# Two attention layers and two feed-forwards on one core: the first feed-forward's matmuls in three rounded parts, and copies and sums of the second half in another order

## The reference, cut to what matters

```python
x = x + L0_xattn(layernorm(x), ctx)   # attention over features, 8 heads, a band of +-64; gated by ctx
x = x + L0_ffn(layernorm(x))          # only the 32 best of the 64 positions of each row
x = x + L1_xattn(layernorm(x), ctx)   # 32 heads in 8 groups, keys and values from ctx
x = x + L1_ffn(layernorm(x))          # squared relu, plus a gate-weighted expert, layer norm after it

def L0_ffn(x):
    scores = x @ w_r + b_r
    idx = top_k(scores, 32)           # per row
    h = gelu(x[idx] @ w1 + b1)        # 256 -> 1024
    return zeros.at[idx].set(h @ w2 + b2)   # 1024 -> 256
```

## Time and profile before

| what | us |
|---|---|
| median of 3 runs (334.99 to 337.39) | 335.25 |
| the profiled execution | 335.92 |
| its span in the profile | 334.2 |
| what lies outside the span (335.92 - 334.2) | 1.7 |
| TensorE, busy | 309.2 |
| VectorE, busy | 237.7 |
| ScalarE, busy | 198.6 |
| GpSimd, busy | 181.4 |

### The profile page before, as it was taken

The page is one execution under the profiler, slowest core; times in us unless marked ns, Lnnn a source line. Parts: engine busy times, 40 slices in busy tenths (PEclk is TensorE's granted clock), DMA queues, the critical chain, the costliest instruction groups (busy, mean ns, idle before and its releaser), DMA issues.

```text
span 334.2 us, 7216 instructions
## 1 busy us (share of the span) xinstructions
PE 309.2 (93%) x2178; PEld 241.2 (72%) x2178; DVE 237.7 (71%) x921; ACT 198.6 (59%) x415; POOL 181.4 (54%) x294
## 2 busy tenths in 40 slices
PE   6997989998999999999998998879899999999992
PEld 4976667676777777776687875657666578888892
DVE  6778889999999999984246156755788647662264
ACT  4758988887777787868531324566678944104210
POOL 6648566677776957577514414243443831336643
PEclk9999999999999999999999999999999999999999
DMA  6999020202010101100000000000000000000000
GB/s 194 365 372 341 8 49 2 50 1 49 3 41 8 38 13 28 26 1 3 2 0 0 2 0 0 0 2 1 2 1 2 0 2 0 3 32 15 19 31 31
DMA packets 13302, 14.51 MB, mean 43 GB/s; under 512 B 2513, under 2 KB 11985, under 8 KB 13265
## 3 DMA queue, kind: packets, MB, share of 16 engines
q1 hardware_dynamic: 12688, 13.72, 13.0%
q10 hardware_dynamic: 576, 0.33, 0.3%
HBM read 10.64 MB, written 1.05 MB: 35 GB/s over the span
## 4 chain that ended last, share of the span: by engine, by line
PE 61%; POOL 13%; DVE 11%; issue 8%; ACT 6%; POOLq 0%; DVEq 0%; ACTq 0%
PE S L772 6%; PE S L432 5%; PE O L459 5%; PE ST L443 4%; PE ST L797 4%; PE S L566 4%; PE S L648 2%; PE S L715 2%; POOL rstd L1081 2%; POOL hT L1097 2%; PE PJ L692 2%; DVE masked L1294 2%; PE O L729 2%; PE PJ L395 2%; PE O L597 2%
## 5 line engine op out<-in xcount | busy, mean ns | idle before, releaser
L1294 DVE CUSTOM_DVE_ANT_0 masked<-S,band 128x192 bf16<-128x192 f32 x256 | 79.6, 353 | 8.9 <-PE S L432 6.9
L893 ACT ACTIVATE ex<-ST 128x384 f32<-128x384 f32 x128 | 60.9, 491 | 17.7 <-PE ST L443 16.3
L1078 POOL TENSOR_SCALAR rstd<-mv 128x1 f32<-128x1 f32 x40 | 12.1, 303 | 76.1 <-DVE mv L1231 75.5
L432 PE MATMUL S<-qk 128*128 128x384 f32 x128 | 52.1, 408 | 0.8 <-DVE mw L1294 0.4
L443 PE MATMUL ST<-qk 128*128 128x192 f32 x256 | 48.1, 271 | 2.5 <-ACT ex L893 2.0
L443 PEld LDWEIGHTS ST<-qk 128*128 128x128 f32 x256 | 44.9, 189 | 5.0 <-issue 4.4
L1138 POOL TENSOR_SCALAR_AFFINE_SELECT ex<-ex 128x512 f32<-128x512 f32 x32 | 20.4, 639 | 29.6 <-ACT ex L893 29.5
L459 PE MATMUL O<-ex,v 128*32 128x192 f32 x512 | 34.1, 338 | 0.0
L432 PEld LDWEIGHTS S<-qk 128*128 128x128 f32 x128 | 24.1, 188 | 13.3 <-issue 11.4
L1426 DVE TENSOR_REDUCE mw<-S 128x8 f32<-128x512 f32 x32 | 22.0, 686 | 13.0 <-PE S L648 13.0
L863 ACT ACTIVATE hs<-PJ,sb,byhead 128x512 fp32r<-128x512 f32 x29 | 22.6, 779 | 11.5 <-PE PJ L396 10.6
(11 more groups left out here) (204 smaller groups left out, 720.6 us busy)
## 6 DMA issues: line engine op xcount, KB each, us to landing
qk<-kp SPq DMA_DIRECT2D x48, 48.0 KB
w<-in_w SPq DMA_DIRECT2D x2, 1024.0 KB, 10.0
cx<-in_cx SPq DMA_DIRECT2D x1, 1024.0 KB, 9.7
up<-in_up SPq DMA_DIRECT2D x1, 1024.0 KB, 11.8
down<-in_down SPq DMA_DIRECT2D x1, 1024.0 KB, 10.9
out<-x SPq DMA_DIRECT2D x8, 128.0 KB, 1.7
cxT<-in_cxT SPq DMA_DIRECT2D x1, 768.0 KB, 6.1
x<-in_x SPq DMA_DIRECT2D x1, 768.0 KB, 7.9
```

The costliest lines, as they stand in the source:

```text
L432: mm(out, r32(qp[:, t % 2, g, b, P * c:P * c + P]), r32(mv_), start=True, stop=True).then_inc(s["pe_s"], 1)
L893: A(ex[:, (n // 2) % 4, 2 * w:2 * w + 2, :], ST[n % 2][:, 0:2 * WIN].rearrange("p (h k) -> p h k", h=2), ACT.Exp, scale=SCALE).then_inc(s[ ...
L1294: last = V.tensor_tensor_reduce(out=masked[:, n % 2, h, :], in0=S[n % 2][:, WIN * h:WIN * h + WIN], in1=band[:, c, :], scale=1.0, scalar=N ...
```

## The change

1. The matmuls of `ffn_up` and `ffn_down` run in three rounded parts: high x high, high x low and low x high, where high is the value rounded to fp32r and low the rest. 64 fp32 matmuls become 192 rounded ones of the same 256 columns. The parts have to be made:
   - of the up weights by ScalarE (a copy of 128 x 512 at l = 10 of tiles 2 to 5) and GpSimd (a subtract at l = 13 of the same tiles), into the new `w1s`; of the down weights by ScalarE (four casts, in slots (7,12), (7,14), e = 12 and e = 13) and VectorE (subtracts at e = 2, 3, 13, 14), into a free part of `qk`;
   - of the gathered tokens by ScalarE and VectorE, for tiles 0 to 3 at once in tile 7's slots 2 and 3, for tiles 4 to 7 one by one at each `take` (one copy and one subtract more);
   - of the hidden layer by ScalarE after every gelu (a copy into a ring of four buffers in `qk`) and VectorE (`ffn_low`, a subtract one slot later).
2. The steps stand in other slots: tables `UP0`, `GELU0`, `DOWN0` for the first half; up and gelu of the second half at e = 31 to 38 and its downs at e = 34 to 41 (n = -14 to -7); scatters at e = 29, 31, 43, 44, so that all eight stand ahead of n = 0; `ffn_out` at e = 28 and 42.
3. VectorE, not GpSimd, normalises tiles 6 and 7 for the choice.
4. In the second attention L1032 moves from the end of a slot to its start on ScalarE, and the exponential's table load from n = 2 to n = -6. GpSimd's sum `x` + beta moves from the last stage into the second attention's slots (n = 21 + 4t, into `cx`). The gate's two VectorE instructions of tiles 5 to 7 move ahead of the tile before's final instruction.
5. The second feed-forward's weights are loaded into `w1` and `w2` once their parts have been made, not into buffers of their own at the start.

The core of the diff:

```diff
+        SCATTER = {29: (0, 1), 31: (2, 3), 43: (4, 5), 44: (6, 7)}
+        UP0, GELU0 = (9, 10, 13, 14, 16, 18, 20, 22), (11, 12, 13, 14, 16, 18, 20, 22)
+        DOWN0 = (15, 17, 19, 21, 23, 25, 26, 27)
...
-                for k in range(2):
-                    last = mm(up_bank(f), w1[:, k, P * f:P * f + P], xsT[:, k, T * half:T * half + T], start=(k == 0), stop=(k == 1))
+                for i, (k, a, b) in enumerate(PARTS):
+                    last = mm(up_bank(f), r32(w1s[:, a, k, P * f:P * f + P]), r32(x_part(g, b)[:, k, :]),
+                              start=(i == 0), stop=(i == len(PARTS) - 1))
...
-                last = mm(down_bank(c), hT[:, f, P * c:P * c + P], w2[:, f, :], start=(f == 0), stop=(f == FC - 1))
+                pe.wait_ge(s["f_lo"], FC * g + f + 1)
+                for m in range(2):
+                    for i, (a, b) in enumerate(((0, 0), (1, 0), (0, 1))):
+                        last = mm(down_bank(2 * g + m), r32(ffn_h(f, a)[:, P * m:P * m + P]), r32(w2s[:, f, b, :]),
+                                  start=(f == 0 and i == 0), stop=(f == FC - 1 and i == 2))
...
+                A(hT[:, f, 0:T], up_bank(f), ACT.Gelu_apprx_tanh, bias=b1[:, f:f + 1]).then_inc(s["fa_up"], 1)
+                if m >= 4:
+                    act.wait_ge(*ring_last(m))
+                A(r32(ffn_h(f, 0)), hT[:, f, 0:T], ACT.Copy).then_inc(s["fa_hi"], 1)
...
+            def ffn_low(g, f):
+                dve.wait_ge(s["fa_hi"], FC * g + f + 1)
+                V.tensor_tensor(r32(ffn_h(f, 1)), hT[:, f, 0:T], ffn_h(f, 0), ALU.subtract).then_inc(s["f_lo"], 1)
...
-                    dve.wait_ge(s["pool_fxn"], t + 1)
+                    if t < TILES - 2:
+                        dve.wait_ge(s["pool_fxn"], t + 1)
+                    else:
+                        dve.wait_ge(s["f_rstd"], t + 1)
+                        normalise(x_norm(t), t, "dve_fxn")
...
-                if n == 2:
+                if n == -6:
                     A(warm[:, :], ident[:, 0:1], ACT.Exp)
+                for i in (0, 3):
+                    p = at(n, SPREAD[i] + 1, 8, PAIRS)
+                    if p is not None:
+                        act.wait_ge(s["gp_e"], 4 * p + i + 1)
+                        A(stacked(p, i), S[1][:, :].rearrange("p (g t q) -> p g t q", g=2, t=4), ACT.Copy).then_inc(s["ga_q"], 1)
...
+                t = at(n, 21, 4, TILES)
+                if t is not None:
+                    pool.wait_ge(s["g_x"], t + 1)
+                    G.tensor_tensor(cx[:, t, :], x[:, t, :], vecs[:, 4, :], ALU.add).then_inc(s["h_xb"], 1)
...
+                if 4 <= t < TILES - 1:
+                    moe_gate(t + 1)
                 dve.wait_ge(s["h_y"], 2 * t + 2)
```

More of the change, by code:

```diff
@@ L94, in build @@
         wf1 = sb("wf1", [P, 2, T])
-        up = sb("up", [P, 2, DF])
-        down = sb("down", [P, FC, T])
+        w1s = sb("w1s", [P, 2, 2, DF])
         eg = sb("eg", [P, 2, T + NEXP])
@@ L408, in slot_ @@
             def slot_(T_, l):
-                f = UP_FIRST.get(UNITS * T_ + l, tail_up(T_, l))
-                if f is not None and UNITS * T_ + l not in (END + 11, END + 12):
-                    ffn_up(0, f)
-                for i in tail_down(T_, l):
-                    ffn_down(0, i // FC, i % FC)
+                feed_forward(since_end(T_, l))
                 t, r = T_, l
@@ L1404, in ffn_add @@
                 V.tensor_tensor(x[:, t, :], scatter_bank(t), x[:, t, :], ALU.add).then_inc(s["f_x"], 1)
-            for T_, l in SLOTS_ALL:
-                slot_(T_, l)
             def slot1(n):
-                c = at(n, -4, 8, 2)
-                if c is not None:
-                    ffn_out(2 + c)
+                e = n + AHEAD
+                if e > 30:
+                    if tail_gelu(e - 1):
+                        ffn_low(*tail_gelu(e - 1))
+                    if e == 42:
+                        ffn_out(2)
+                        ffn_out(3)
                 t = at(n, 21, 4, TILES)
```

297 lines of the change are left out of this document (185 added, 112 removed).

## The result

The changed kernel takes 338.94 us (median of 8 runs, 337.02 to 339.99), the kernel before in the same comparison 335.88 (8 runs, 334.99 to 337.39). The ratio is 1.008, with a 95% interval of 1.0052 to 1.0109: slower by 0.8%, where 332.2 was forecast. The profiled execution took 339.97 us with a span of 338.2, 4.0 more than the span of before. It is the second slowest of the eight; their mean granted clocks lie between 0.982 and 0.989, where the profiled execution of before had 0.999.

What follows compares the result with a forecast made beforehand. TensorE was taken as nearest to a bound everywhere, except the second attention, where list order decides. Even stretch 0, tail and second half -0.1, copies -2.2, end -0.7: -3.0 from 335.92, so 332.9, median 332.2; range 328.0 to 337.5.

Steps and rivals of the forecast that it cites:

- B: Even stretch: making the up weights' parts on ScalarE and GpSimd fits into their free time; 0 taken, ends 0 and 7.6.
- C: Tail, 160 to 181: later osb copy, cheaper normalise, one more gather copy; second half starts +0.3 us, ends -2.3 and +4.9.
- F: End: with gate ahead and beta added earlier, the last tile's sum waits only for the last down matmul; -0.7 us.
- A: Feed-forward on TensorE: 192 rounded matmuls (23.0 us) replace 64 fp32 ones (27.6); 4.6 us go, 2.3 per half.
- Rival 2: Second half: TensorE's saving comes through as the first maximum isn't held by hs; -6.2 us, 329.0; chance 0.23.
- The bound of 7.6: Even stretch: upper end in us, were every ScalarE copy and GpSimd subtract of the up weights on the path.
- if the cover is gone: Even stretch: an exponential's mask would wait behind a GpSimd subtract of 1.28 in one tile, +1.3 us each.
- So no term below comes from it: All stretches: the granted clock is 1.00, so no term of the forecast was given to it.
- D: Second half and first scores, 181 to 212: first score 203.05, first maximum 205.0; -0.1 by n = 7, ends -3.6 and +1.3.
- E: Second attention: with ScalarE's copies L1032 earlier, L715's waits on TensorE shrink; -2.2 us, ends -2.5 and 0.
- Rival 3: Tail: ScalarE's gelu and copy pairs delay tile 7's path, second half 4.9 late; +1.6 us, 336.9; chance 0.15.
- SBUF — State Buffer: Second half: port pair shared by VectorE and GpSimd could hold up to four `ffn_low`, 2.8 us; nothing taken, 0.7 in range.

Runs made afterwards that it cites:

- e10: e8 with only the high x high part of every up and down product on TensorE, 64 matmuls instead of 192: 330.45 us, ratio 0.9815.
- e8: Changed kernel with the edits of e3, e5 and e6, and the copies of the fourth spread head behind hs again: 332.85 us, ratio 0.9923.
- e7: Kernel before, fp32 feed-forward kept, with first spread head's copies and table load earlier, VectorE's normalise of tiles 6 and 7, and gate ahead: 331.57 us, ratio 0.9881.
- e1: Changed kernel without GpSimd's four subtracts of the up weights, high weights used in place of the low ones: 336.95 us, ratio 1.0018.
- e5: Changed kernel with GpSimd's subtract in tiles 3 to 5 made to wait for VectorE's selection of its slot: 337.22 us, ratio 1.0055.
- e9: e8 with ScalarE's last two casts of the down weights, and VectorE's subtracts of them, in later slots: 331.58 us, ratio 0.9846.
- e3: Changed kernel with the first bias add ahead of tile 7's rank and the first two scatters ahead of its selection: 336.88 us, ratio 1.0037.
- e6: Changed kernel with GpSimd's sums x + beta back in the last stage: 339.85 us, ratio 1.0116.
- e2: Changed kernel with 13 unread 128 x 128 matmuls on TensorE where it waits for the choice of tile 7: 337.03 us, ratio 1.0044.
- e4: Kernel before with only ScalarE's spread-head copies at the start of their slot and the exponential's table load at n = -6: 333.34 us, ratio 0.9939.
- e11: e8 with 18 unread 128 x 128 matmuls on TensorE in the four slots around the second attention's first score: 334.01 us, ratio 0.9915.

## Why the prediction was wrong

Two steps failed: B took nothing for GpSimd's subtracts, which cost 2.4 us, and no term had the clock, which cost 2.7. Smaller misses lie in C and in the sums moved for F.

- **A, TensorE's work: the size was right, its worth was not.** Six matmuls of an up step take 0.71 in the chain of the changed kernel, 0.12 each. But e10 shows that the first half waits little for TensorE (0.7 of 7.7 us at the up step, 1.4 at tile 7's transposed scores), and e8 against e7 that with everything mended the rounded parts and their making lose 1.3 us. Rival 2 is refuted: with hs ahead again, e8 has the eighth maximum 34.07 behind the first up step, before 34.64, and not 3.6 sooner.
- **B, the parts made in the even stretch: this step failed first.** "ScalarE has 20 us free and GpSimd 31, ... I take 0": free time of the engine was the wrong test. The subtract fitted into GpSimd's gap and held VectorE, which is full there: 0.8 a tile, 2.4 us (e1, e5). The bound of 7.6 held it, but the value was taken from the wrong end, and the price "if the cover is gone" was named for another wait.
- **C, the tail.** The osb copy was said to come 1.5 later, the cause ScalarE's list; it came 4.8 later, 2.4 of them from B. ScalarE's list has 1.1 of the rest (e9: two casts fewer, 0.9 earlier). The other 1.3 came ahead of it, with tile 5's score, where C had no term. The normalise gave 0.58 by e7 (0.84 said). The wait ahead of the first up step was said to grow by 0.27; it grew by 1.76: the order of scatters, sums and the low part on VectorE (0.6 to 0.8, e3 and e6) and the clock (0.9, e2). I had counted instructions there and not read VectorE's list between the gather and the up step.
- **"So no term below comes from it"** (the clock) **failed next.** The denser list has less to put into the wait for tile 7's choice, TensorE idles, and its clock falls: 2.7 us in the profiled execution. No rival had it.
- **D had the number at full clock, and its reason in part.** From the first up step to the first maximum I had 205.0 - 181.35 = 23.65; e3 measures 23.99. In it the first score comes 22.36 behind the up step, 21.70 said and 21.99 before: the denser list did not close the waits of this stretch. The maximum stands 1.63 behind its score, 1.95 said and 0.65 before; hs is the reason, as said, but its order costs only 0.4 in all (e4 against e7). e8's 23.55 is no test of it, as hs is ahead again there. To the eighth maximum the changed kernel gains 1.42 on before, which gives the 1.3 of the late maximum back, as said.
- **E and F were right.** -2.2 said, -2.3 alone (e4) and -2.9 in the changed kernel; -0.7 said, -0.70 measured. But the moved sums, which F counted as a help, cost 0.9 on VectorE before the last stage (e6); the edit was given no price at all.
- **Rival 3** had the place and the size (the second half 4.9 late; 5.0 measured) with the wrong mechanism: ScalarE's pairs are a part of it, the subtracts and the clock are most.
- **The Trainium skill's "SBUF — State Buffer", weighed in D,** was the right page at the wrong place. I tried the shared pair against `ffn_low`, where one of the sixteen was held (at 188.76, 0.94 for 0.42, beside the key products), and not against the four subtracts and eight sums that GpSimd itself was given, though the trace had VectorE's 1.12 beside a GpSimd instruction.

The missed terms are 2.4 (B), 2.7 (clock), 0.8 (scatters) and 0.9 (sums), 6.8 together; with the forecast's -3.0 that is +3.8, where the two traces differ by +4.0. That this comes so near is partly luck: 0.8 lost up to tile 7's transposed scores, where C had 0.1, and 0.7 that E gained beyond its 2.2 cancel in it.

## What to carry to other kernels

A gap in one engine's list is not free room: before work is put into it, read what the other engines do at that moment, and look for instructions that already take longer beside each other than alone, as VectorE's 1.12 beside GpSimd did in the trace of before. Work saved on the engine that is busiest is worth only what its next wait leaves of it; where that wait is for a chain on other engines, the saving becomes idle, and idle can cost the clock. When a stage is made denser, the order in which its consumers wait (a sum ahead of the operand that everything waits for) has to be read again, list by list.

## What the runs showed of the hardware that was not expected

- GpSimd's subtract of 128 x 512 stretches a VectorE selection of 128 x 128 from 0.35 to 1.23 us, and a wait that moves them apart takes that away at a cost of 0.1 (e5). GpSimd's instructions, too, are longer beside some of VectorE's, though no run moves these apart. In the changed kernel, GpSimd's timeline beside VectorE's subtract of the down weights, and beside its keys at 159.74:

```profile
157.16 0.96 POOL L1203 TENSOR_SCALAR_AFFINE_SELECT ex<-ex 128x256 f32<-128x256 f32 x1
157.18 0.66 DVE L1474 TENSOR_TENSOR qk<-w,qk 128x512 fp32r<-128x512 f32 x1
...
159.93 1.68 POOL L1159 TENSOR_SCALAR hT<-x,mv,rstd 128x256 f32<-128x256 f32 x1
162.17 0.59 POOL L1203 TENSOR_SCALAR_AFFINE_SELECT ex<-ex 128x256 f32<-128x256 f32 x1
```

  In the kernel before, the same mask and the same normalise, and VectorE's keys:

```profile
154.27 0.42 POOL L1140 TENSOR_SCALAR_AFFINE_SELECT ex<-ex 128x256 f32<-128x256 f32 x1
...
156.50 1.25 POOL L1097 TENSOR_SCALAR hT<-x,mv,rstd 128x256 f32<-128x256 f32 x1
...
156.86 0.75 DVE L1394 SCALAR_TENSOR_TENSOR kp<-cxT,given,xs 128x512 fp32r<-128x512 f32 x1 [2.48 <-ACT xs L928]
```

  Here normalise and keys overlap as well and neither is longer than elsewhere (1.25 and 0.74): with GpSimd's instruction first nothing was held, with VectorE's first GpSimd's was. One pair each way is no rule.
- Useless matmuls in a gap made the kernel faster where the slow clock ran dense work (e2), and slower where they outlasted the gap (e11). Whether the clock falls differs between executions of one kernel. The eight of the changed kernel have mean clocks of 0.982 to 0.989. The kernel before falls too: of its thirty executions beside e1 to e4, the six with 0.985 took 336.77 to 337.34 us, the 21 with 0.995 and above 334.76 to 335.69. No trace of such a one is kept, so where its clock falls is open.
